# Recurrent loop of a fused kernel: new order of products and activations, and beta times state on VectorE

## The reference, cut to what matters

```
LSTM, each step:   a = x_t Wx + b + h Wh;  i, f, o = sigmoid(a[0:3]);  g = tanh(a[3])
                   c = f c + i g;  h = o tanh(c)
delta cell, each step (8 heads, S is 32 x 32 for each batch and head):
    xp = silu(h W_in);  k, v, q, beta = projections of xp
    kn        = k / (|k| + 1e-6)
    retrieved = S kn
    delta     = v - retrieved
    S         = tanh(beta * S + delta kn^T)
    out       = (S q) * silu(S q)
rnn, each step:    h = tanh(x_t Wx + b + h Wh)
```

## Time and profile before

| | us |
|---|---|
| median of 3 runs | 3473.64 (3473.26 to 3475.56) |
| the profiled execution, its own time | 3478.83 |
| its span from the first to the last instruction | 3477.0 |
| PE busy | 2897.3 (83%) |
| PE weight load busy | 2164.5 (62%) |
| VectorE busy | 1842.8 (53%) |
| ScalarE busy | 1110.5 (32%) |
| GpSimd busy | 761.8 (22%) |
| of it L574, beta times state, 512 instructions | 360.5 |
| mean granted TensorE clock, share of full speed | 0.641 |

### The profile page before, as it was taken

One profiled execution on the slowest core, in us unless ns is written; L12 is line 12 of the kernel. 1 busy time (PEld: TensorE's weight loads), 2 busy tenths in 40 slices (PEclk: granted clock), 3 DMA queues, 4 the chain that ended last, 5 costly groups with the idle time before them and its releaser, 6 DMA issues. The chain is left out here.

```text
span 3477.0 us, 94868 instructions
## 1 busy us (share of the span) xinstructions
PE 2897.3 (83%) x35915; PEld 2164.5 (62%) x35915; DVE 1842.8 (53%) x7177; ACT 1110.5 (32%) x4414; POOL 761.8 (22%) x1477
## 2 busy tenths in 40 slices
PE   6899999956888894689899899888547789999998
PEld 3557888844555663456666666665314578888755
DVE  3534444464435433456656656654375854444577
ACT  1233222221222232334444444443223432222222
POOL 1111111102200001344544544545101211111000
PEclk9996555556997795555555555555558955555699
DMA  1000000000000001343343343343000000000000
GB/s 74 2 2 0 0 0 0 0 33 1 2 2 0 1 0 58 66 98 71 66 98 71 66 98 71 65 98 71 37 0 1 2 0 0 0 0 0 0 0 12
DMA packets 106860, 101.37 MB, mean 29 GB/s; under 512 B 95616, under 2 KB 95616, under 8 KB 97536
## 3 DMA queue, kind: packets, MB, share of 16 engines
q1 hardware_dynamic: 106624, 98.13, 12.9%
HBM read 89.68 MB, written 8.39 MB: 28 GB/s over the span
## 5 line engine op out<-in xcount | busy, mean ns | idle before, releaser
L574 POOL TENSOR_TENSOR l2r_beta_s<-l2r_state,l2r_beta_f 128x256 f32<-128x256 f32 x512 | 360.5, 725 | 543.8 <-ACT l2r_state L479 528.5
L695 DVE TENSOR_TENSOR l2r_pre<-l2r_o_ps,l2r_beta_s 128x256 f32<-128x256 f32 x512 | 193.4, 419 | 246.0 <-PE l2r_o_ps L374 245.9
L479 ACT ACTIVATE l2r_state<-l2r_pre 128x256 f32<-128x256 f32 x512 | 190.7, 417 | 260.0 <-DVE l2r_pre L695 260.0
L327 PEld LDWEIGHTS l2r_lstm_ps<-l2r_h_ring,l2r_w_part 128*128 128x128 bf16 x3072 | 103.6, 105 | 222.4 <-DVE l2r_h_low L681 220.9
L362 PE MATMUL l2r_d_ps<-l2r_state,l2r_kq 128*32 128x128 f32 x2056 | 206.8, 421 | 36.4 <-ACT l2r_state L479 36.3
L327 PE MATMUL l2r_lstm_ps<-l2r_h_ring,l2r_w_part 128*128 128x8 bf16 x3072 | 123.4, 169 | 121.7 <-DVE l2r_h_low L681 121.7
L374 PE MATMUL l2r_o_ps<-l2r_rows,l2r_outer 32*128 32x128 f32 x2048 | 207.8, 496 | 15.9 <-DVE l2r_rows L687 15.9
L469 ACT ACTIVATE l2r_lstm_ps<-l2r_lstm_ps 128x24 f32<-128x24 f32 x256 | 44.8, 175 | 392.0 <-PE l2r_lstm_ps L327 391.9
L340 PEld LDWEIGHTS l2r_r_ps<-l2r_r_ring,main_even_layers 128*128 128x128 f32 x512 | 128.8, 311 | 59.3 <-issue 47.1
L340 PE MATMUL l2r_r_ps<-l2r_r_ring,main_even_layers 128*128 128x8 f32 x512 | 149.3, 365 | 9.7 <-ACT l2r_r_ring L487 9.7
L133 PE MATMUL l3r_acc<-l3r_xw,main_base 128*128 x512 | 154.7, 389 | 1.6 <-issue 1.6
(11 more groups left out here) (534 smaller groups left out, 7565.1 us busy)
## 6 DMA issues: line engine op xcount, KB each, us to landing
l2r_beta_f<-l2r_beta_store SPq DMA_DIRECT2D x256, 256.0 KB, 6.1
main_odd_layers<-in_l SPq DMA_DIRECT2D x1, 4826.5 KB, 14.3
l2r_beta_store<-l2r_beta_tok SPq DMA_DIRECT2D x256, 8.0 KB, 1.5
main_odd_layers<-in_l SPq DMA_DIRECT2D x1, 3672.0 KB, 16.0
l2r_v_store<-l2r_v_part SPq DMA_DIRECT2D x128, 24.0 KB, 2.0
l2r_v_rows<-l2r_v_store SPq DMA_DIRECT2D x16, 192.0 KB, 6.3
main_decay<-in_decay SPq DMA_DIRECT2D x1, 3072.0 KB, 11.3
main_even_layers<-in_l SPq DMA_DIRECT2D x1, 2762.5 KB, 9.3
```

What stands on the lines that cost most here:

```text
L327: last = nc.tensor.matmul(lstm_ps[:, at + g * B:at + (g + 1) * B], w_part[k][:, g * P:(g + 1) * P], h, start=False, stop=(m == 2), skip_gr ...
L479: nc.scalar.activation(state[:, h * 2 * P:(h + 1) * 2 * P], pre[:, h * 2 * P:(h + 1) * 2 * P], ACT.Tanh).then_inc(state_ready[h], 1)
L574: nc.gpsimd.tensor_tensor(beta_s[:, half], state[:, half], beta_f[:, q % BETA_SLOTS, n % QUARTER, half], ALU.mult).then_inc(s["bs_ready"], 1)
L695: nc.vector.tensor_tensor(pre[:, half].rearrange("p (c n) -> p c n", c=2), o_ps[:, 2 * h:2 * h + 2, 0:P], beta_s[:, half].rearrange("p (c ...
```

## The change

- PE: in each step the rnn product stands right behind retrieve, the spread of delta before the LSTM's products, and in step 0 all bias and input products of the LSTM behind the spread.
- ScalarE: rnn tanh, new state, and then the LSTM's gates and tanh.
- VectorE: beta times state (`kept`) ahead of the mask; h of the step before and its split between the mask and the sum; projections and output reductions behind the sum; the cell last.
- GpSimd: no longer makes beta times state.
- For the first 31 steps of the LSTM (`IN_BANK = 31`), h is split by two VectorE instructions in SBUF (`split_alone`), and PE waits for each of the three parts by itself.

```diff
@@ PE, lstm_products @@
-                    pe.wait_ge(s["low_ready"], n + 1)
-                    for m, h in enumerate((high(h_ring[:, (n - 1) % SLOTS, :]), h_mid[:, :], h_low[:, :])):
+                    alone = n <= IN_BANK
+                    if not alone:
+                        pe.wait_ge(s["low_ready"], n + 1)
+                    h_parts = high(h_ring[:, (n - 1) % SLOTS, :]), high(h_rest[:, :]) if alone else h_mid[:, :], h_low[:, :]
+                    for m in range(3):
+                        if alone:
+                            pe.wait_ge(s[("h_ready", "rest_ready", "low_ready")[m]], n + 1)
@@ PE, the loop @@
-                        if lstm is not None and lstm >= 1 and step == 0:
-                            lstm_bias(lstm)
-                            lstm_inputs(lstm, 0)
-                        elif lstm is not None:
-                            lstm_products(lstm * TC + step)
+                        if rnn is not None and step >= 1:
+                            rnn_product(rnn * TC + step)
                         if delta is not None:
                             spread_delta(n)
-                        if lstm is not None and lstm >= 1 and step == 0:
-                            for g in range(1, 4):
-                                lstm_inputs(lstm, g)
-                            lstm_products(lstm * TC)
-                        if rnn is not None:
-                            if step == 0:
-                                rnn_inputs(rnn)
-                            rnn_product(rnn * TC + step)
+                        if rnn is not None and step == 0:
+                            rnn_inputs(rnn)
+                            rnn_product(rnn * TC)
+                        if lstm is not None:
+                            if lstm >= 1 and step == 0:
+                                lstm_bias(lstm)
+                                for g in range(4):
+                                    lstm_inputs(lstm, g)
+                            lstm_products(lstm * TC + step)
@@ ScalarE, the loop @@
-                        if lstm is not None:
-                            lstm_gates(lstm * TC + step)
+                        if rnn is not None:
+                            rnn_tanh(rnn * TC + step)
                         if delta is not None:
                             new_state(delta * TC + step)
                         if lstm is not None:
+                            lstm_gates(lstm * TC + step)
                             lstm_tanh(lstm * TC + step)
-                        if rnn is not None:
-                            rnn_tanh(rnn * TC + step)
@@ GpSimd: kept and its call are gone; VectorE has them @@
+                def kept(n):
...
+                    for h in range(2):
+                        half = slice(h * 2 * P, (h + 1) * 2 * P)
+                        dve.wait_ge(state_ready[h], n + 1)
+                        nc.vector.tensor_tensor(beta_s[:, half], state[:, half], beta_f[:, q % BETA_SLOTS, n % QUARTER, half],
+                                                ALU.mult).then_inc(s["bs_ready"], 1)
@@ VectorE, split of h in the first 31 steps @@
+                def split_alone(n):
+                    h = h_ring[:, n % SLOTS, :]
+                    dve.wait_ge(s["h_ready"], n + 2)
+                    nc.vector.tensor_tensor(h_rest[:, :], h, high(h), ALU.subtract).then_inc(s["rest_ready"], 1)
+                    dve.wait_ge(s["rest_ready"], n + 2)
+                    nc.vector.tensor_tensor(h_low[:, :], h_rest[:, :], high(h_rest[:, :]), ALU.subtract).then_inc(s["low_ready"], 1)
@@ VectorE, the loop @@
+                        if rnn is not None and step == 0:
+                            add_out(rnn)
+                        if delta is not None:
+                            kept(n)
                         if delta is not None or final:
                             masked(n)
-                        if rnn is not None and step == 0:
-                            add_out(rnn)
+                        before = k * TC + step - 1
+                        if IN_BANK <= before < T:
+                            lstm_h(before)
+                        if IN_BANK <= before < T - 1:
+                            split_h(before)
+                        if delta is not None:
+                            summed(n)
                         if proj is not None:
                             project(proj, step)
                         if out is not None:
                             output(out, step)
-                        if delta is not None:
-                            summed(n)
                         if lstm is not None:
-                            lstm_cell(lstm * TC + step)
-                            lstm_h(lstm * TC + step)
-                        if lstm is not None and lstm * TC + step + 1 < T:
-                            split_h(lstm * TC + step)
+                            lstm_cell(before + 1)
+                            if before + 1 < IN_BANK:
+                                lstm_h(before + 1)
+                                split_alone(before + 1)
```

More of the change, by code:

```diff
@@ L301, in recurrent_stages @@
         BODIES = NTC + 4
+        IN_BANK = 2 * TC - 1
         def waves(k):
@@ L560, in _ @@
                         if lstm is not None:
+                            lstm_gates(lstm * TC + step)
                             lstm_tanh(lstm * TC + step)
-                        if rnn is not None:
-                            rnn_tanh(rnn * TC + step)
             @block.gpsimd
             def _(pool):
-                def kept(n):
-                    q = n // QUARTER
-                    if n % QUARTER == 0:
-                        pool.wait_ge(beta_loaded[q % BETA_SLOTS], 16 * 4 * (q // BETA_SLOTS + 1))
-                    for h in range(2):
-                        half = slice(h * 2 * P, (h + 1) * 2 * P)
-                        pool.wait_ge(state_ready[h], n + 1)
-                        nc.gpsimd.tensor_tensor(beta_s[:, half], state[:, half], beta_f[:, q % BETA_SLOTS, n % QUARTER, half],
-                                                ALU.mult).then_inc(s["bs_ready"], 1)
                 def spread(src, mask, slots, which, g, h, t0, count):
@@ L639, in _ @@
                     for step in range(TC):
-                        if delta is not None:
-                            kept(delta * TC + step)
                         if proj is not None:
@@ L671, in split_h @@
+                def split_alone(n):
[4 more added lines that the diff above has]
+                    nc.vector.tensor_tensor(h_low[:, :], h_rest[:, :], high(h_rest[:, :]), ALU.subtract).then_inc(s["low_ready"], 1)
                 def split_h(n):
                     at = n % TC * 4 * B
+                    count = n - IN_BANK + 1
@@ L673, in split_h @@
                     rest = lstm_ps[:, at:at + B]
+                    nc.vector.tensor_tensor(lstm_ps[:, at + 3 * B:at + 4 * B], lstm_ps[:, at + 2 * B:at + 3 * B], tanh_c[:, :],
+                                            ALU.mult).then_inc(s["h_psum"], 1)
                     dve.wait_ge(s["h_ready"], n + 2)
-                    dve.wait_ge(s["h_psum"], n + 1)
+                    dve.wait_ge(s["h_psum"], count)
                     nc.vector.tensor_tensor(rest, lstm_ps[:, at + 3 * B:at + 4 * B], high(h_ring[:, n % SLOTS, :]),
@@ L772, in _ @@
                 nc.vector.tensor_copy(selv_bf[:, :], sel_v).then_inc(s["consts_ready"], 1)
[L773 to L777 removed]
+                split_alone(-1)
                 for k in range(BODIES + 1):
```

27 lines of the change are left out of this document (11 added, 16 removed).

## The result

The changed kernel takes 3492.47 us (median of 5 runs, 3488.94 to 3493.93) against 3473.64 (5 runs, 3472.09 to 3477.85): ratio 1.0052, 95% interval 1.0039 to 1.0064. It is slower by 18.8 us, where 17 less were forecast. The profiled execution took 3493.93 (span 3492.1), its granted clock in the loop 0.50 as before.

A forecast was written before the change was run, and what follows sets the result against it. No engine is full; one closed chain through both recurrences sets 3.93 us a step. Start -16.2, body 2 -1.9, 13 bodies +1.3 and the last two -0.5 make -17.3: 3473.64 to 3456 us, range 3432 to 3484.

The forecast's parts named there:

- Plain step 3.68: A loop step without extra work takes 3.68 us in place of 3.93, with VectorE's own queue as the last wait.
- start -16.2: While the LSTM runs alone, products start sooner after h, 0.77 us a step; 16.2 us saved ahead of the first L717.
- Step 6: Two table loads of 1.28 us around the square root, now ahead of the new state, add 0.65 us a body.
- Step 0: Bias and four input products of 2.12 us stand whole between spread and LSTM products, adding 2.2 us a body.
- Steps 12 to 15: Output products on PE, and step 15's sum into x ahead of beta times state, add 0.5 us a body.
- Contention: VectorE's beta times state waits for running GpSimd instructions after steps 8, 9 and 11: 1.0, 0.2, 0.5, together +1.7 us a body.
- rival B: Each half of beta times state waits for its own GpSimd instruction after steps 8, 9, 11; 3484 us; B and slower 0.17.
- Body 2: Body 2 has neither reductions nor GpSimd's L620, so it gets 1.9 us shorter.
- bodies 16 and 17: Bodies without LSTM, whose loop of 3.26 us holds beta times state in its shade; -0.5 us for both.
- Worth nothing by itself: Taking 360 us of beta times state off GpSimd gains nothing by itself, since nobody waited for that engine.
- Rival C: The wait for the values returns in each body, a floor of 64 us; costs nothing at 65.7; no chance given.
- the ring: Closed chain of waits tying the LSTM and delta recurrences together, 3.93 us a step before; it can't go below 3.26.

The follow-up runs named there:

- e6: Kernel before with only the new start: h's split in SBUF and three separate waits for the first 31 LSTM steps; 3454.69 us, ratio 0.9954.
- e1: Changed kernel plus a one-element sigmoid, result unread, right behind the square root; 3476.75 us, ratio 1.0005 to the kernel before.
- e2: Changed kernel with step 0's rnn input products and rnn product moved ahead of delta's spread on TensorE; 3482.76 us, ratio 1.0028 to before.
- e4: Changed kernel with step 12's transpose moved on VectorE ahead of the delta cell's sum; 3486.29 us, ratio 1.0031 to the kernel before.
- e8: Changed kernel with the output cell's square moved from GpSimd to ScalarE; 3477.96 us, ratio 1.0027 to the kernel before.
- e3: Changed kernel with beta times state moved back to GpSimd, in its old place; 3454.80 us, ratio 0.9938 to the kernel before.
- e5: e3 with the edits of e1 and e2 added; 3431.03 us, ratio 0.9875 to the kernel before.
- e12: e5 with the load of the values issued right behind their store; 3392.20 us, ratio 0.9775 to the kernel before.
- e11: e10 with the load of the values issued right behind their store; 3445.89 us, ratio 0.9928 to the kernel before.
- e10: Changed kernel with the four edits of e1, e2, e4 and e8, beta times state on VectorE; 3436.40 us, ratio 0.9901 to the kernel before.
- e9: e5 with the values loaded right behind their store and e4's transpose edit; 3381.81 us, ratio 0.9744 to the kernel before.

## Why the prediction was wrong

- **Plain step 3.68, LSTM-alone step 2.0, start -16.2, first keys to first values 29: right.** They are 3.69, 2.02, -15.1 and 30.0; e6 gives -15.4 for the start by itself.
- **Step 6, "two table loads, +0.65": this step failed most.** It took the number of loads from the earlier trace rows as fixed, while the change alters which function comes first behind the square root. There are three loads, step 6 is 2.26 over the plain step and so 1.6 a body over the forecast; e1 gave 19.3 back.
- **Step 0, "bias and four input products of 2.12": failed by misreading the change.** The diff puts the rnn's inputs and product behind the spread as well, 0.95 in 12 bodies (e2).
- **Steps 12 to 15, "+0.5": too small.** They added 1.2. The cost of PE's products was counted, not that the transpose ahead of them had moved behind the sum (e4: 0.56 of it).
- **Contention, "+1.7": about right in sum, wrong in place.** Step 8 holds 1.4 of it, since both halves wait there; this is rival B's mechanism at one of its three places (e8 gave 1.1 a body back). Step 9 has nothing and step 11 0.15, where 0.2 and 0.5 were forecast. That the sum came out near is partly luck. The cell's product (L746, now L756) fell from 1.19 to 0.72, not "still 1.2": now it is GpSimd that waits. The product starts at 1924.46, amid four spreads of keys, and one of those takes 1.195 where their median is 0.746. The product's timeline row, and the line view of the spreads, 1910 to 1930 us (ns min/median/max):

```profile
1924.46 0.72 DVE L756 TENSOR_TENSOR l2r_cell<-l2r_sq_sq,l2r_sq_sig 128x512 f32<-128x512 f32 x1
...
L573 POOL TENSOR_TENSOR l2r_kq<-l2r_knt_f,main_even_layers x4: 738/746/1195, 1922.5 to 1924.6; 128x256 f32<-128x256 f32 x4
```

- **Body 2 "-1.9", bodies 16 and 17 "-0.5":** they are -0.9 and +6.5. Body 2 has the third table load too (step 6 5.70 instead of 3.93). In bodies 16 and 17 step 12's wait for the transpose is there without the LSTM (4.57 instead of 3.45), as is step 8's (4.38 and 4.00 instead of 3.25). The forecast also had no wait for the values there: PE waits for them 1.4 at the end of body 2 and 1.9 at the end of body 16, whose step 15 takes 4.96 instead of 3.45.
- **"Worth nothing by itself", of GpSimd's relief: not contradicted, but it left the other side uncounted.** The forecast never priced the same order with beta times state left where it was. That is 3.25 instead of 3.69 in a plain step (e3) and no collision in step 8, 43 us of stage together. This is no error of the sum, which had these 3.68 and the collision in it; it is the comparison that would have spoken against this half of the change.

The differences close: bodies 3 to 15 took 33.9 more (1.3 forecast), the last two 6.5 more (-0.5), body 2 0.9 less, the start 15.1 less; together 24.4, against -17.3 forecast. Rival B named the right sign and nearly the right time (3484), but its mechanism is only one of the four causes, and at one place of three, so its nearness is mostly luck. Rival C's wait for the values is what e3 and e5 ran into, with bodies of 61.7 to 66.9 about its floor of 64, until the load was moved.

## What to carry to other kernels

For each instruction that a reordering puts behind another, ask which engine waits for its result, not only what it costs its own engine: the transpose, the rnn's inputs and the tanh behind the square root were all cheap where they stood. Before work is moved onto an engine of the ring, price the new order with that work left where it is. And once a ring is faster, look at transfers issued late in a queue for no reason: moving one line of SyncE's order took 35 us off the stage with beta times state on GpSimd (e12 against e5), more than anything in the change gave, and nothing with it on VectorE (e11 against e10).

## What the runs showed of the hardware that was not expected

- The table that a tanh brings in behind a square root does not serve the sigmoid; the one that a sigmoid brings in serves both. Each load is 1.28 us, and the activation follows 1.30 after its start.
- An operation that is made in two instructions can be blocked twice: 2.02 for a pair of 0.75 (1.18 and 0.92 where one alone is 0.42), as GpSimd's next instruction gets in between.
- In such a collision either engine can be the one that waits: VectorE's product of 128x512 before, which started 0.06 behind a spread (1.19 against 0.69), GpSimd's spread now, which started 0.13 behind the product (1.195 against 0.746). In both the later one was held up, so their order decides whether the ring waits or an engine that nobody waits for.
- A load of 192 KB lands 6.6 us after its issue in the median when four loads of 256 KB are issued right ahead of it (e5), and 2.9 when they come behind it (e9).
